# TensorE's windowed-attention batches in one loop over all layers, the mask laid by 64 rows a bank, the norm floor on ScalarE, and new orders

## The reference

```
for i in range(6):
    x = attn_layer(shift_tokens(x), ...) + x      # 16 heads of 64, windows of 32 tokens
    x = ffn_layer(shift_tokens(x), ...) + x       # layer norm, 128 -> 2*341, a * gelu(gate) -> 128
attn_layer:
    q, k, v = split(x @ Wqkv)                     # 128 -> 3*1024
    q, k = l2norm(q) * qs, l2norm(k) * ks         # t / max(norm(t), 1e-12)
    q, k = rotary(q, scale), rotary(k, 1/scale)
    sim = q . k * 8, masked to the own window and the one before
    out = softmax(sim) . v ;  out @ Wo
```

## Time and profile before

| | |
|---|---|
| runs | 4111.69, 4117.26, 4122.36 us |
| profiled execution | 4119.48 us, span 4117.7 us, mean granted clock 0.974 |
| TensorE matmul busy | 3683.9 us, 89% |
| VectorE busy | 3504.1 us, 85% |
| ScalarE busy | 2524.8 us, 61% |
| GpSimd busy | 1584.1 us, 38% |
| first and last projection of the stack | 705.3 and 4045.1 us |

### The profile page before, as it was taken

The page is one execution under the profiler, slowest core; times in us unless marked ns, Lnnn a source line. Parts: engine busy times, 40 slices in busy tenths (PEclk is TensorE's granted clock), DMA queues, the critical chain, the costliest instruction groups (busy, mean ns, idle before and its releaser), DMA issues. The chain is left out here.

```text
span 4117.7 us, 121951 instructions
## 1 busy us (share of the span) xinstructions
PE 3683.9 (89%) x49057; PEld 2077.1 (50%) x49312; DVE 3504.1 (85%) x4692; ACT 2524.8 (61%) x3292; POOL 1584.1 (38%) x1115
## 2 busy tenths in 40 slices
PE   5888885799998999998999989999989999899997
PEld 2333331455555555555555545555555555555553
DVE  6888885789998898988898988899979899899894
ACT  3666663465666565656666656666656666566663
POOL 3222231434343444443444434444434343344441
PEclk8999997899999999999999999999999999999998
DMA  1000001111112111112111111111121111111112
GB/s 27 1 1 1 1 1 57 41 37 25 37 25 53 36 32 30 34 29 58 27 36 27 36 53 30 33 31 32 31 58 25 37 25 37 51 32 31 32 31 57
DMA packets 60615, 131.31 MB, mean 32 GB/s; under 512 B 15748, under 2 KB 31624, under 8 KB 60168
## 3 DMA queue, kind: packets, MB, share of 16 engines
q1 hardware_dynamic: 60168, 124.11, 12.5%
HBM read 23.62 MB, written 4.19 MB: 7 GB/s over the span
## 5 line engine op out<-in xcount | busy, mean ns | idle before, releaser
L1024 PE MATMUL slot<-w_qkv,xs 128*128 (+1 forms) x2304 | 1109.8, 612 | 104.4 <-issue 75.1
L750 POOL TENSOR_TENSOR half_sq<-sq 128x1024 f32<-128x1024 f32 x192 | 501.1, 2610 | 1575.5 <-ACT sq L890 1566.1
L755 POOL TENSOR_TENSOR cosq<-cosq,sinq 128x1024 f32<-128x1024 f32 x384 | 901.8, 2365 | 364.4 <-DVE sinq L799 363.3
L1024 PEld LDWEIGHTS slot<-w_qkv,xs 128*128 128x128 f32 x2304 | 410.6, 193 | 525.2 <-issue 493.4
L890 ACT ACTIVATE sq<-slot 128x1024 f32<-128x1024 f32 x384 | 391.9, 1021 | 409.8 <-PE slot L1024 409.8
L797 DVE TENSOR_TENSOR cosq<-slot,table 128x1024 f32<-128x1024 f32 x384 | 467.4, 1217 | 190.7 <-ACT sq L890 175.5
L826 DVE TENSOR_TENSOR qk<-cosq,ry 128x1024 f32<-128x1024 f32 x384 | 474.2, 1245 | 0.6 <-ACT ry L945 0.6
L799 DVE TENSOR_TENSOR sinq<-slot,table 128x1024 f32<-128x1024 f32 x384 | 465.8, 1213 | 0.0
L978 PEld LDWEIGHTS slot<-ident,qk 128*128 128x128 f32 x3072 | 350.4, 142 | 227.7 <-issue 137.7
L978 PE MATMUL slot<-ident,qk 128*128 128x128 f32 x3072 | 396.6, 275 | 48.4 <-DVE qk L826 44.3
L373 DVE TENSOR_REDUCE at_rowmax<-at_slot 128x1 f32<-128x512 f32 x512 | 317.3, 683 | 51.4 <-PE at_slot L460 49.7
(11 more groups left out here) (124 smaller groups left out, 5514.1 us busy)
## 6 DMA issues: line engine op xcount, KB each, us to landing
vb<-va SPq DMA_DIRECT2D x720, 130.0 KB, 2.3
w_qkv<-in_w_qkv SPq DMA_DIRECT2D x21, 512.0 KB, 5.6
w_o<-in_w_o SPq DMA_DIRECT2D x6, 512.0 KB
w<-in_w SPq DMA_DIRECT2D x6, 342.0 KB
res<-in_x SPq DMA_DIRECT2D x4, 512.0 KB, 6.0
kept<-res SPq DMA_DIRECT2D x1, 2048.0 KB, 8.7
out<-fin_res SPq DMA_DIRECT2D x8, 256.0 KB, 2.5
w<-in_w SPq DMA_DIRECT2D x6, 171.0 KB
```

The costliest lines, as they stand in the source:

```text
L750: nc.gpsimd.tensor_tensor(half_sq[:, :, :], squares[:, :, 0, :], squares[:, :, 1, :], ALU.add).then_inc(S["folded"], 1)
L755: nc.gpsimd.tensor_tensor(cosq[:, side], cosq[:, side], sinq[:, side], ALU.add).then_inc(S["qk"[side] + "_added"], 1)
L1024: last = nc.tensor.matmul(slot(kind, n)[:, i, :], xs[:, n * P:(n + 1) * P], w_qkv[:, (0 if layer is None else layer) % 2, "qkv".index(kind ...
```

## The change

All edits lie in `windowed_stack` and its tables.

```diff
 PE_ORDER = stages(
-    "q0 k0 qT3- kT3- r2- s3- vb2- k1 va2- kT0 q1 qT0 v0 r3- k2 va3- vb3- s0 q2 wo- qT1 r0 v1 kT1 centre- vb0 va0 "
-    "var- q3 v2 s1 k3 qT2 h0- kT2 h1- r1 h2- s2 vb1 v3 va1 y- ")
+    "k0 q0 qT3- kT3- r2- s3- vb2- k1 va2- r3- q1 vb3- va3- v0 kT0 q2 qT0 k2 s0 wo- qT1 kT1 r0 v1 centre- vb0 s1 "
+    "var- q3 qT2 va0 k3 r1 h0- kT2 h1- s2 h2- va1 v2 vb1 v3 y- ")
...
 ACT_ORDER = stages(
...
+    "next- v3- square_k0 exp2- square_q0 qT3- kT3- r2- norm0 exp3- square_k1 r3- square_q1 v0 kT0 qT0 square_k2 "
...
 POOL_ORDER = stages(
-    "fold1- add_q1- add_k1- add_q2- fold2- add_k2- fold3- add_q3- add_k3- fold0 add_k0 add_q0 ")
+    "fold2- add_q2- add_k2- fold3- add_q3- add_k3- fold0 add_k0 add_q0 fold1 add_q1 add_k1 ")
...
-        ident16 = sb("ident16", [P, P], BF16)
+        pair16 = sb("pair16", [P, 2, DH], BF16)
...
             step(0, 0, 0, 0, False)
-            align()
-            with eng.Fori(1, BATCH) as b:
-                step(b, 0, b, 1, True)
-            with eng.Fori(1, DEPTH) as l:
-                step(l * BATCH, l, 0, BATCH, True)
-                align()
+            if order is PE_ORDER:
+
+                eng.addr_align(FETCH)
+                with eng.Fori(1, DEPTH * BATCH) as unit:
+                    step(unit, unit // BATCH, None, 1, True)
+            else:
                 with eng.Fori(1, BATCH) as b:
-                    step(l * BATCH + b, l, b, BATCH + 1, True)
+                    step(b, 0, b, 1, True)
+                with eng.Fori(1, DEPTH) as l:
+                    step(l * BATCH, l, 0, BATCH, True)
+                    with eng.Fori(1, BATCH) as b:
+                        step(l * BATCH + b, l, b, BATCH + 1, True)
...
-            nc.vector.tensor_copy(ident16[:, :], ident[:, :]).then_inc(S["const_ready"], 1)
+            for r in range(2):
+                rows = slice(DH * r, DH * r + DH)
+                nc.vector.tensor_copy(pair16[rows, :, :], ident[rows, None, rows].broadcast_to([DH, 2, DH])).then_inc(
+                    S["const_ready"], 1)
...
-                    link(nc.vector.reduce_sum(ss[:, :], half_sq[:, :, :], AX.X), "floor")
-                    nc.vector.tensor_tensor(ss[:, :], ss[:, :], least[:, :], ALU.max).then_inc(S["sumsq"], 1)
+                    nc.vector.reduce_sum(ss[:, :], half_sq[:, :, :], AX.X).then_inc(S["sumsq"], 1)
...
-                    nc.scalar.activation(logs[:, :], ss[:, :], ACT.Ln).then_inc(S["log_link"], 1)
-                    act.wait_ge(S["log_link"], unit * TPB + n + 1)
+                    nc.scalar.activation(logs[:, :], ss[:, :], ACT.Relu, bias=minus_least[:, 0:1]).then_inc(S["log_link"], 1)
+                    act.wait_ge(S["log_link"], 2 * (unit * TPB + n) + 1)
+                    nc.scalar.activation(logs[:, :], logs[:, :], ACT.Ln, bias=least[:, 0:1]).then_inc(S["log_link"], 1)
+                    act.wait_ge(S["log_link"], 2 * (unit * TPB + n) + 2)
...
                 for r in range(2):
-                    nc.tensor.matmul(slot("s", t)[:, r, :], ident16[:, :], mask[:, 0 if t == 0 else 1, :],
+                    rows = slice(DH * r, DH * r + DH)
+
+                    nc.tensor.matmul(slot("s", t)[:, r, :], pair16[rows, :, :].rearrange("p a n -> p (a n)"),
+                                     mask[rows, 0 if t == 0 else 1, :],
                                      start=True, stop=False, skip_group_check=True)
...
-                    if n == 0 and starts is not None:
-                        pe.wait_ge(S["w_" + kind], 16 * (starts + 1))
+                    if n == 0:
+                        pe.wait_ge(S["w_" + kind], 16 * (layer + 1))
                         passed(pe)
...
-                    wait_ff(pe, starts, layer)
+                    pe.wait_ge(S["w_ff"], 16 * W_FF * (unit // BATCH + 1))
+                    passed(pe)
```

More of the change, by code:

```diff
@@ L587, in windowed_stack @@
         logs = sb("logs", [P, 2 * HEADS])
-        least = sb("least", [P, 2 * HEADS])
+        least = sb("least", [P, 1])
+        minus_least = sb("minus_least", [P, 1])
         ry = sb("ry", [P, 2 * HEADS])
@@ L608, in windowed_stack @@
         S = {n: sem("ws_" + n) for n in list(EVENTS) + ["const_loaded", "const_ready", "w_q", "w_k", "w_v", "qks_loaded", "w_ff", "tables",
-                                                        "cleared", "xs_ready", "floor_link", "s_link", "va_link", "vb_link", "log_link", "rstd_link", "passed"]}
+                                                        "cleared", "xs_ready", "s_link", "va_link", "vb_link", "log_link", "rstd_link", "passed"]}
         vb_ready = [sem(f"ws_vb_ready{t}") for t in range(TPB)]
@@ L612, in windowed_stack @@
         W_FF = 5
-        CONSTS = 6
+        CONSTS = 7
         block = ctx.enter_context(nc.Block())
@@ L650, in step @@
                     if looped or 0 <= first - back < DEPTH * BATCH:
-                        batch = b if back == 0 else (BATCH - 1 if starts is not None else b - 1)
+                        batch = b if back == 0 or b is None else (BATCH - 1 if starts is not None else b - 1)
                         before = []
@@ L659, in step @@
                     layer_end(it, l)
-            def align():
-                if order is PE_ORDER:
-                    eng.addr_align(FETCH)
             step(0, 0, 0, 0, False)
-            align()
-            with eng.Fori(1, BATCH) as b:
-                step(b, 0, b, 1, True)
-            with eng.Fori(1, DEPTH) as l:
-                step(l * BATCH, l, 0, BATCH, True)
-                align()
-                with eng.Fori(1, BATCH) as b:
-                    step(l * BATCH + b, l, b, BATCH + 1, True)
+            if order is PE_ORDER:
[3 more added lines that the diff above has]
+            else:
+                with eng.Fori(1, BATCH) as b:
+                    step(b, 0, b, 1, True)
[3 more added lines that the diff above has]
+                        step(l * BATCH + b, l, b, BATCH + 1, True)
             step(DEPTH * BATCH, None, BATCH, DEPTH * BATCH, False)
@@ L732, in _ @@
                 pool.memset(k[:, :, :], 0.0).then_inc(S["cleared"], 1)
-            for buffer, value in ((ones, 1.0 / D), (zero, 0.0), (epsc, EPS), (least, 1e-24), (xs, 0.0), (xs2, 0.0)):
+            for buffer, value in ((ones, 1.0 / D), (zero, 0.0), (epsc, EPS), (least, 1e-24), (minus_least, -1e-24), (xs, 0.0), (xs2, 0.0)):
                 pool.memset(buffer[:, :], value).then_inc(S["cleared"], 1)
-            pool.wait_ge(S["cleared"], 10)
+            pool.wait_ge(S["cleared"], 11)
             nc.gpsimd.tensor_tensor(centring[:, :], ident[:, :], ones[:, :], ALU.subtract).then_inc(S["cleared"], 1)
-            pool.wait_ge(S["cleared"], 11)
+            pool.wait_ge(S["cleared"], 12)
             for v in (va, vb):
```

## The result

The changed kernel takes 4154.0 us (median of 4, 4147.4 to 4157.2) against 4119.8 beside it: ratio 1.0083, interval 1.0062 to 1.0105. The forecast was 3971 us, faster than before; it is 0.8% slower, outside the range.

What follows compares the result with a forecast made beforehand. TensorE in its fixed order was taken to set the pace, VectorE close behind, with a hole at layer starts. From 4119.5 us, -66 for one loop, -80 for the units and -2.2 for the median gave 3971 us, range 3893 to 4042.

Steps and rivals of the forecast that it cites:

- the sum for a unit: One pass of TensorE's loop: 68.0 us less 1.7 gives 66.3 us, so -80 us over 47 units.
- One loop, -66: TensorE's layer starts: waits and slow clock there vanish with a single loop, -66 us, between -55 and -70.
- I take nothing for them; the cover is `y`: Unit start on TensorE: added weight waits and address instructions hide behind `y`'s 2.6 us; at worst 0.5 us a unit.
- a sign of being wrong: Wrong if "issue" stands ahead of `k0` with more than 1 us in each unit, or units stay at 68.
- that 0.5 is gone: Behind the scores of tile 2: `h2` and others now precede the values, removing a wait of 0.5 us.
- Mask, -0.15: Two mask matmuls on different rows and banks may overlap: -0.15 us a unit, between -0.85 and +0.7.
- the 0.7 for shape changes: TensorE, mask term: six more changes of tile shape a unit at 0.12 us each, +0.7 us.
- Norm floor, nothing: L818 leaves VectorE, whose busy time falls from 61.7 to 57.5 us a unit; worth nothing by itself in the sum.
- New orders: Order placed by hand: waiting falls from 4.0 to 2.35 us a unit, -1.65, including 1.15 for ScalarE's copies.
- a third: Tile 1's paired scalings caught by GpSimd's `fold2`: 1.3 us would reach TensorE at `kT1`; 0.4 us counted.
- The waits only move: Rival: L818's wait for GpSimd becomes L826's, units 67.6 us, 4038 us; chance 0.20 shared with the hole staying.
- Slower: the one loop pays at its end: Rival: the loop's way back costs 7.4 us more in all 47 units, 4320 us; decides from 3.1 a unit; chance 0.06.

Runs made afterwards that it cites:

- the repaired run: Changed kernel with TensorE's loop cut behind `wo`, laid 32 slots into its block, and GpSimd's fold of tile 2 held until `scale_k1` is done: 3934.7 us, 0.9584.
- the run with the cut: Changed kernel with TensorE's one loop cut behind `wo` instead of behind `y` and laid 32 slots into its block, fold not held: 3998.3 us, 0.9717.
- offset 24: Changed kernel with TensorE's loop laid 24 instruction slots further into its block of 256, nothing else: 4095.9 us, 0.9954.
- the last run: Kernel with loop cut behind `wo` and fold of tile 2 held, laid 200 slots into its block in place of 32: 4109.6 us, 0.9995.

## Why the prediction was wrong

The step that failed is the sum for a unit: 66.3 us, where 70.4 were measured. It put nothing for instructions that come late within the body, which cost 1.6 us; it took 0.3 us for the loop's end, which cost 1.36; and it took 0.4 us for a lock that costs 1.06. So the 80 us to be gained in the units became a loss of some 98.

*One loop, -66.* The long entries went, and the clock's dips with them, but the loop alone is worth 47 us (0.9893), below the stated bound of 55. Two things were mis-sized. The 70.2 us set down to the layer starts came from the 68.0 of layer 5 alone; against the 68.2 of all ordinary intervals it is 61. And the sentence on what the loop adds, "I take nothing for them; the cover is `y`", up to 0.5 us a unit, failed: `y`'s 2.6 us don't cover the branch. It takes 0.87 us a unit with the old tables and 1.36 with the new ones, which is over the 1 us that the prediction had named as a sign of being wrong. I had named the place and the cover and sized it from the 0.30 of one row, where the 40 ordinary entries of before average 0.61.

*The missing term.* The sum had nothing for instructions that come late inside the body. It is the largest error, 1.6 us a unit. It was there to be read: the 1.85 us of scores in the earlier trace rows against 1.48, and their 1.97 us to `vb1`, I took for a wait that goes with the order ("`h2` and others stand between `s2` and the values: that 0.5 is gone"). Within those 1.85 us the 118th pass starts 0.35 us late. In other units of before the same wait has a record of its own, 11 passes before the end of the scores (timeline, TensorE, before):

```profile
979.90 0.33 PE L993 MATMUL slot<-kT,qT 64*32 64x64 f32 x11 [0.67 <-issue]
```

That is 117 passes, 234 slots in, the seventh boundary by the same count. The new order puts `r1` before `kT2` and leaves one pair of feed-forward products, the mask and 242 slots of scores in the block; 0.5 us became 1.6. The cut and the offset together repair both terms: 4154 to 3998 us.

*Mask, -0.15.* The overlap is full, as in its bound, and the gain 0.3 us a unit by the run without it. The size was about right, but partly by luck: the 0.7 for shape changes is not shown, and 0.3 of what was given back went into waits that the sum didn't have.

*Norm floor, nothing.* 0.3 us a unit; "L818 goes" and VectorE's fall to 57.6 of 69.3 us in a stretch of the changed kernel's inner units came as said.

*New orders.* The placing by hand holds where no instructions were late: in the repaired run only ScalarE's copies are waited for, 0.73 us and not 1.15 with 0.2. That its 65.4 us a unit lie near the forecast's 66.3 less the lock, the loop's end and the jitter (65.3) is luck in part: 64.7 of them are work, where the working had 63.9. The lock was put at "a third" of 1.3; it happens in every unit, 1.06. The sum's 66.3 for a unit compares with 66.8 for the run with the cut, which has this lock.

*The rivals.* "The waits only move" had the lock and its place. In the changed kernel two scalings take 4.25 us beside the fold and 2.35 with the fold held back: it happened in 48 of 48 units, and I gave it one chance in three. The Trainium skill's rule on the shared port (SBUF — State Buffer, SBUF: two separate sides) says that one of the two engines stands while the other holds it; the trace agrees. "Slower: the one loop pays at its end" had the right sign and place, with 7.4 us where 1.36 stand; the 3.1 us a unit from which it decides were passed only because a second fetch wait and the lock joined it (70.4 - 66.3 = 4.1).

The Trainium skill (Runtime: NRT & Kernel Launch, Instruction fetch mechanics) says that instructions come in blocks of 256, that crossing into the next costs little, "mostly hidden", and that a taken branch out of the pages held forces a fetch. The trace agrees with the size of the block (places that move by 12 and 32 passes for 24 and 64 slots) and with the branch (1.36 us, which end 1.9 to 2.3 us after a packet). At six of the seven boundaries in a unit of the changed kernel TensorE doesn't wait, and the trace agrees that the crossing is hidden. It does not where the block holds little but quick passes: 1.6 us at the seventh, and some 170 us in all by the offset alone.

*Open.* The changed kernel's units are 0.6 us longer than the run with the cut and the two fetch waits explain (66.8 + 1.4 + 1.6 = 69.8 against 70.4). With offset 24 the wait in the scores stays where the packet began late, and why it does in these units isn't known. What makes a packet late isn't settled, though in the last run the longest waits go with the weight loads; nor was it tried to cut the loop at another place than `wo` at the same offset, so cut and offset are told apart by the rows, not by a run each.

## What to carry to other kernels

An "issue" wait in the middle of a run of equal matmuls was, in all these kernels, the program coming late. Count the slots from the aligned loop top, two to a pass, and look for a boundary there; lay the loop so that no block is filled by small, quick matmuls, and put the branch behind the longest queued work. Any change of order moves these places, so a reordered kernel should be compared at two or three offsets before its order is judged. The same holds for an experiment that moves the code: look whether another wait went or came with it. And where two instructions of different engines that can lock one another are placed by hand within each other's time, put the collision in at its full price: all units are alike, so it came in each of the 48, and when other waits moved by a microsecond it shrank in all of them.

## What the runs showed that was not expected

One number, the offset of the loop in its block, moved the same program from 3934.7 to 4109.6 us (0.9584 to 0.9995 of the kernel of before). A body of 1980 slots fetches nine blocks each time round, one more than it touches, so nothing of it is kept from one unit to the next. And where no instruction came late, units lay within 0.5 us of one another (66.80 to 67.24); the spread of before (67.6 to 69.7), which I had booked as jitter of 0.3 us, goes with its fetch waits, those in the scores and those at the loop's end, which alone are 0 to 1.08 us from unit to unit (correlation of an interval with the sum of its "issue" waits: 0.96).
